# Layer 0 of a modulated convolution in five matmuls instead of six, with the next block's first half copied into a stacked buffer

## The chip, the cores and the metric

The kernel runs on one core of one Trainium2 chip. The metric is the device time of one launch in microseconds (us). The engines are TensorE (PE; its weight loads are shown apart as PEld), VectorE (DVE), ScalarE (ACT), GpSimd (POOL) and SyncE (SP, which here only issues transfers).

## What is computed

The input `x` is (128 samples, 32 channels, 512 positions). It goes through four modulated 1-D convolutions (3 taps, 32 to 32 channels), then through a mixture of experts with a shared expert, and is added to the result. Cut to what matters here:

```python
TYPES = ('same', 'upsample', 'same', 'downsample')
def _conv_same(x, w):
    p = (K - 1) // 2
    return lax.conv_general_dilated(x[None], w, (1,), [(p, p)], ...)[0]
def _layer(x, style, w, b, mw, mb, typ):
    s = style @ mw.T + mb
    weight = SCALE * w * s[:, None, :, None]
    demod = lax.rsqrt(jnp.sum(weight * weight, axis=(2, 3)) + EPS)
    weight = weight * demod[:, :, None, None]
    if typ == 'same':
        out = jax.vmap(_conv_same)(x, weight) + b[None, :, None]
...
x = x + _L0_ffn_ref(_L0_cond_ref(x, cond_512, ...), ...)   # 16 experts, top 4 of each row, and a shared expert
```

The layer of the change is the first one, of type "same": each output position takes the three input positions around it.

## The kernel before

**Tiling.** The 4096 rows (sample, channel) are cut into G = 32 blocks of 128 rows, which are four samples of 32 channels. For the convolutions the 512 positions of a row are split by their remainder modulo Q = 4. The 128 partitions then hold four groups of 32 channels, one for each remainder, and the free dimension holds 4 samples of V = 128 positions each. In this layout a convolution is a matmul with a 128x128 matrix of placed taps: in layer 0 the matrix `FIRST` takes the inputs of the same group of four positions, and `FIRST + 1` takes those of the following group (the data shifted by one column). Of this second matrix only the rows of the first two remainders, partitions 0 to 63, hold taps.

**Two parts.** All operands of TensorE are split into a high and a low part (`x0[0]`, `x0[1]` for the data, `cwt[0]`, `cwt[1]` for the taps), and a product is three matmuls: high by high, high data by low taps, low data by high taps. Layer 0 therefore takes six matmuls of 128x512 for each block (`hi_passes` issues four, `lo_passes` two). The data's high part is made by ACT (`first_in`, L586, out of `xraw`), its low part by DVE (`first_in`, L840).

**Order.** Each engine runs its own program, `body(g)` for g = 0 to 33, and semaphores tie them together. In body g of PE stand, in this order: layer 0 of block g+1, the transposes of block g-2's rows, layer 1 of block g, layer 3 of block g-1, the shared expert's first product, layer 2 of block g, then the router's logits and the shared expert's second product. For the last six blocks the shared expert is put off until the convolutions are through. ACT takes each layer out of its bank (L592) and makes the high part of block g+2's input; DVE makes the low parts. Layer 0 of block 0 and layer 0 of block 1 have nothing of a block before them; block 1's stands in body 0. In body 0 DVE also mixes the taps of the last layer (`mixture`, L865 and L867), which ACT copies (L572) ahead of its evacuation of layer 2.

**SP's queue.** SP issues nearly all transfers, in one order. In body g: an output block (L377) and a load of `xbase` (L379), four copies that stack layer 0's result for layer 1 (L362), four writes of the finished rows `h_rows` (L385), and the load of `xraw` for block g+3 (L390). An instruction that waits on SP holds up all that stand behind it. Ahead of the bodies SP waits until layer 1's input of block 0 is stacked, and then loads `xraw` of block 2 (L370). In body 1 it also loads the first expert's weights, 1.5 MB (L396, L397).

After the convolutions the experts' jobs run, with TensorE at work nearly all the time to the end.

The functions that the diff touches, and what calls them:

Of the kernel before, what the change touches and what calls it, by code (L numbers as in the profile page):

```python
# [5 lines left out]
P = 128  # L6
F32 = mybir.dt.float32
# [10 lines left out]
def mk_adaln_ffn(nc, x, xq, styleT, taps, placed_taps, small, modT, gateT, Wup, Wdn, Sup, Sdn, out):  # L18
# [46 lines left out]
    with ExitStack() as ctx:  # L65

        def sb(name, shape, dt=F32):
            buffer = ctx.enter_context(nc.sbuf_tensor(name, shape, dt))
            size = 2 if dt == BF16 else 4
            for n in shape[1:]:  # L70
                size *= n
            if 0 < size % 64 <= 32:
                ctx.enter_context(nc.sbuf_tensor(f"{name}_gap", [P, 8], F32))
            return buffer

        def sem(name):
# [56 lines left out]

        x0 = [sb("x0_hi", [P, NB, VP], F32R), sb("x0_lo", [P, NB, VP], F32R)]

        x1p = sb("x1p", [P, 2, NB, V], F32R)


# [62 lines left out]
        names = ("style_loaded taps_loaded placed_loaded0 placed_loaded1 placed_loaded2 bias_loaded gate_loaded iota_done consts_done dve_step mixed_ready pos_ready "  # L201
                 "s_psum wts_hi wts_lo dem_psum sqrt_done eps_ready s_ready s2_ready scales_ready "
                 "raw_loaded w_hi w_lo fill_written "
                 "x_loaded0 x_loaded1  base_loaded0 base_loaded1 x0_hi x0_lo "
                 "l0_done l1_done l2_done l3_done t1_ready t2_ready t3_ready h_ready "
                 "x1_ready x1_stacked x2_ready x3_ready xt_t xt_hi xt_lo up_done sg_ready z_ready "
                 "logits_done sig_ready mask_ready prefix_done place_ready zt_t zt_hi zt_lo down_done "
# [65 lines left out]
        def within(g, least, most):  # L273
            return not isinstance(g, int) or least <= g < most
# [59 lines left out]
        def _(sp):  # L334
# [17 lines left out]
            def stack(g, plane_=None):  # L352
# [4 lines left out]
                for plane, to, part, rows, back in PLACES:  # L357
                    if plane_ is not None and plane != plane_:
# [3 lines left out]
                    sp.dma_start(x1[C * to:C * (to + rows), :, :, plane, dst].rearrange("p a b u -> p (a b) u").bitcast(F32),  # L362
                                 x1p[C * part:C * (part + rows), :, :, src].rearrange("p a b u -> p (a b) u").bitcast(F32)).then_inc(S["x1_stacked"], 16)

            stack(0, 0)
            sp.wait_ge(S["x0_hi"], 1)
            sp.wait_ge(S["x0_lo"], 1)

            sp.wait_ge(S["x1_stacked"], 16 * STACKS)
            sp.dma_start(xraw[:, 0], xq[2]).then_inc(S["x_loaded0"], 16)  # L370

            def body(g, it, u):

                odd = g % 2 if u is None else (R + 1 + u) % 2
                if within(g, 3, G - LATE + 3):
                    sp.wait_ge(S["o_ready"], g - 2)
                    sp.dma_start(out[bass.ds(P * (g - 3), P), :], orow[:, 1 - odd, :]).then_inc(S[f"o_written{1 - odd}"], 16)  # L377
                    if within(g, 3, G + 1):
                        sp.dma_start(xbase[:, 1 - odd, :], x_rows[bass.ds(P * (g - 1), P), :]).then_inc(S[f"base_loaded{1 - odd}"], 16)  # L379
                if within(g, 0, G - 1):  # L380
                    stack(g + 1)
                if within(g, 1, G + 1):
                    sp.wait_ge(S["h_ready"], g)
                    for q in range(Q):
                        sp.dma_start(h_rows[bass.ds(P * (g - 1), P), q * (L // Q):(q + 1) * (L // Q)].rearrange("(b c) w -> c b w", b=NB),  # L385
                                     hrow[C * q:C * q + C, 1 - odd]).then_inc(S[f"h_written{1 - odd}"], 16)
                if within(g, 0, G - 3):
                    sp.wait_ge(S["x0_hi"], g + 2)
                    sp.wait_ge(S["x0_lo"], g + 2)
                    sp.dma_start(xraw[:, 1 - odd], xq[bass.ds(g + 3, 1)].rearrange("a p b v -> p (a b) v")).then_inc(S[f"x_loaded{1 - odd}"], 16)  # L390
                if isinstance(g, int) and g == 1:
                    sp.wait_ge(S["w_lo"], HC + IC)
                    load_expert(0)
# [363 lines left out]
        def _(dve):  # L757
# [71 lines left out]
            def matrix_lo(n):  # L829
                src, at, to, m = MATRICES[n]  # L830
                dve.wait_ge(S["wts_hi"], n + 1 + n // 3)
                minus(cwt[1][:, to:to + m], src[:, at:at + m], cwt[0][:, to:to + m]).then_inc(S["wts_lo"], 1)

            def minus(lo, src, hi):
                return dve.tensor_tensor(lo, src, hi.bitcast(F32), ALU.subtract)  # L835
# [129 lines left out]
            def body(g, it, u):  # L965
# [49 lines left out]
                    dve.tensor_tensor(z[:, 0, :], z[:, 0, :], bank[6][:, I:2 * I], ALU.mult).then_inc(S["z_ready"], 1)  # L1015
                if many:
                    settle(number, many)
                if early and g == G + 1:
                    late_z(G - LATE)
                if is_late(g):  # L1020
# [2 lines left out]
                    routing()  # L1023
                if early and g == 0:
                    mixture(1, 3, PLACED_DOWN, BK, "placed_loaded2", step)
                if within(g, 0, G - 2):
                    first_in(g + 2, odd)
                for ph in range(2):
                    if ph == 1 and shared:
                        dve.wait_ge(S["zt_hi"], g - 1)  # L1030
# [185 lines left out]
        def _(pe):  # L1216
# [29 lines left out]
            def layer0(g):  # L1246
                if isinstance(g, int) and g == 0:
                    pe.wait_ge(S["wts_lo"], 1)
                else:
                    pe.wait_ge(S["t1_ready"], g)  # L1250
                dst = bank[0][:].rearrange("p (b v) -> p b v", b=NB)
                same = [columns(FIRST + m, P, lambda a: x0[a][:, :, m:m + V]) for m in range(2)]
                pe.wait_ge(S["x0_hi"], g + 1)
                hi_passes(pe, dst, same)
                pe.wait_ge(S["x0_lo"], g + 1)
                lo_passes(pe, dst, same).then_inc(S["l0_done"], 1)

            def prefix(number, many):

# [240 lines left out]
def _laid_out(inputs):  # L1500
# [24 lines left out]
        return a.reshape(P, P)  # L1525

    turned = cw.transpose(0, 2, 1, 3)
    placed = [place(turned[0], lambda q, j: j + Q * m - q) for m in range(2)]
    placed += [place(turned[2], lambda q, j: j + Q * m - q - 1) for m in range(2)]
    placed += [place(cw[1], lambda q, j: 1 - 2 * j + q + n) for n in range(4)]  # L1530
    placed += [place(turned[3], lambda q, j: j + Q * m - 2 * q - n) for n in range(4) for m in range(3)]
# [36 lines left out]
```

## Time and profile before

| | |
|---|---|
| median of 3 runs | 1179.65 us (1178.35 to 1181.12) |
| the profiled execution | 1181.02 us, of which the profile's span is 1179.3 us |
| TensorE busy with matmuls | 1122.3 us, 95% |
| VectorE / ScalarE / GpSimd busy | 798.0 / 515.3 / 538.0 us |
| convolution stage | from the start to about 470 us |

The profiled execution is 1.37 us above the median. Its time outside the span is 1.7 us. Busy shares are averages over two stages that differ, so the rows below are read by stretch.

### The profile page before, as it was taken

The page shows a single profiled execution, that of the slowest core. Times are in us where ns is not written, and L with a number is a line of the kernel's source. Part 1 is how long each engine was busy: PE and PEld are TensorE (multiplying, and loading weights), DVE is VectorE, ACT ScalarE, POOL GpSimd, SP SyncE. Part 2 cuts the span into 40 slices and gives each one's busy share as a digit, 9 for nine tenths or more (in the row PEclk, how much of TensorE's full clock was granted, in tenths as well). Part 3 has the DMA queues.
Part 4 walks back from the last instruction along what each step waited for, and adds up shares of the span by engine and source line. Part 5 has one row for each costly group of instructions (what it writes and reads, how often), then busy time and mean ns, then how long its engine had stood idle before and what let it go on. Part 6 is the DMA issues. An engine that isn't in the chain of part 4 may idle for free. (4 is left out here: it accounts for less than half of the span.)

```text
span 1179.3 us, 24615 instructions
## 1 busy us (share of the span) xinstructions
PE 1122.3 (95%) x7157; PEld 1006.7 (85%) x7158; DVE 798.0 (68%) x2057; ACT 515.3 (44%) x1246; POOL 538.0 (46%) x639
## 2 busy tenths in 40 slices
PE   5899999999999978889999999999999999999995
PEld 4788888888888866679999999999997999999995
DVE  7988887888888875745655656556567565555653
ACT  5776666666666653132323333223234232232321
POOL 1000131322222364545566566665655556566663
PEclk8999999999999998979999999999999999999998
DMA  7655555555555541367766776767667776666664
GB/s 253 179 158 157 148 157 158 156 154 143 143 153 152 152 111 44 106 163 147 153 129 114 156 121 125 152 115 154 119 154 160 153 161 122 111 112 109 115 114 71
DMA packets 140255, 163.66 MB, mean 139 GB/s; under 512 B 31456, under 2 KB 97088, under 8 KB 138688
## 3 DMA queue, kind: packets, MB, share of 16 engines
q0 software_dynamic: 36000, 75.39, 35.3%
q1 hardware_dynamic: 102832, 87.06, 25.2%
q10 hardware_dynamic: 1392, 0.85, 0.3%
q8 instruction: 13, 0.21, 0.1%
q14 instruction: 18, 0.15, 0.0%
HBM read 74.58 MB, written 55.18 MB: 110 GB/s over the span
## 5 line engine op out<-in xcount | busy, mean ns | idle before, releaser
L1468 PE MATMUL bank<-xt_hi,wup_hi 128*128 128x256 f32 x1104 | 278.4, 284 | 1.9 <-ACT xt_hi L716 1.5
L1468 PE MATMUL bank<-xt_hi,wup_lo 128*128 128x256 f32 x1104 | 278.1, 284 | 0.0
L445 POOL DMA_INDIRECT lists<-entry,place x128 | 126.0, 984 | 326.8 <-DVE x_lo L835 266.4
L501 POOL DMA_INDIRECT out_rows<-placed,sid x140 | 226.6, 1619 | 90.9 <-DVE placed L1188 66.8
L592 ACT ACTIVATE t<-bank,cB,cA 128x256 f32<-128x256 f32 (+1 forms) x384 | 175.9, 535 | 96.7 <-PE bank L231 89.7
L1468 PEld LDWEIGHTS bank<-xt_hi,wup_hi 128*128 128x128 f32 x1104 | 212.6, 193 | 6.4 <-issue 2.0
L1468 PEld LDWEIGHTS bank<-xt_hi,wup_lo 128*128 128x128 f32 x1104 | 212.9, 193 | 2.5
L486 POOL DMA_INDIRECT placed<-h_rows,gid x140 | 141.5, 1011 | 120.7 <-PE bank L1446 78.2
L1472 PE MATMUL bank<-xt_lo,wup_hi 128*128 128x256 f32 x1104 | 178.3, 284 | 0.0
L1188 DVE TENSOR_SCALAR placed<-bank,all_lists 128x512 f32<-128x512 f32 x138 | 99.8, 748 | 87.0 <-DMA out_rows<-placed,sid 55.2
L733 ACT ACTIVATE zt_hi<-z 128x256 fp32r<-128x256 f32 x138 | 57.6, 418 | 231.0 <-DVE z L1178 231.0
L1472 PEld LDWEIGHTS bank<-xt_lo,wup_hi 128*128 128x128 f32 x1104 | 153.2, 193 | 0.0
L729 ACT ACTIVATE sg<-bank 128x256 f32<-128x256 f32 x138 | 52.4, 380 | 211.6 <-PE bank L1472 211.4
L1484 PE MATMUL bank<-wdn_hi,zt_hi 128*128 128x512 f32 x276 | 114.6, 415 | 2.3 <-ACT zt_hi L733 2.3
L1486 PE MATMUL bank<-wdn_hi,zt_lo 128*128 128x512 f32 x276 | 108.4, 393 | 0.0
L224 PE MATMUL bank<-x_hi,cwt_hi 128*128 128x512 f32 (+1 forms) x256 | 100.3, 395 | 8.3 <-DVE x_hi L1008 3.1
L1484 PE MATMUL bank<-wdn_lo,zt_hi 128*128 128x512 f32 x276 | 107.3, 389 | 0.0
L835 DVE TENSOR_TENSOR zt_lo<-z,zt_hi 128x256 fp32r<-128x256 f32 x138 | 58.8, 426 | 61.9 <-ACT zt_hi L733 61.9
L1178 DVE TENSOR_TENSOR z<-z,bank 128x256 f32<-128x256 f32 x138 | 58.2, 422 | 62.4 <-PE bank L1472 60.9
L224 PE MATMUL bank<-x_hi,cwt_lo 128*128 128x512 f32 (+1 forms) x256 | 99.6, 389 | 0.0
L1160 DVE TENSOR_TENSOR xt_lo<-bank,xt_hi 128x512 fp32r<-128x512 f32 x140 | 90.3, 686 | 11.1 <-ACT xt_hi L716 7.0
L231 PE MATMUL bank<-x_lo,cwt_hi 128*128 128x512 f32 (+2 forms) x384 | 95.2, 355 | 0.0
(258 smaller groups left out, 2088.8 us busy)
## 6 DMA issues: line engine op xcount, KB each, us to landing
x<-x1p SPq DMA_DIRECT2D x63, 384.0 KB
wraw<-in_Wup SPq DMA_DIRECT2D x11, 1024.0 KB, 7.8
xraw<-in_xq SPq DMA_DIRECT2D x32, 260.0 KB, 2.7
xbase<-in_x SPq DMA_DIRECT2D x32, 256.0 KB, 2.8
h_rows<-hrow SPq DMA_DIRECT2D x128, 64.0 KB
x<-x1p SPq DMA_DIRECT2D x63, 127.0 KB
out_rows<-orow SPq DMA_DIRECT2D x30, 256.0 KB, 2.1
wdraw<-in_Wdn SPq DMA_DIRECT2D x11, 512.0 KB, 9.9
```

Source lines behind the costliest of these rows:

```text
L224: r = pe.matmul(dst, lhs[a if data_moves else 0], rhs[0 if data_moves else a], start=n == 0 and a == 0, stop=False)
L231: r = pe.matmul(dst, lhs[0 if data_moves else 1], rhs[1 if data_moves else 0], start=False, stop=last and n == len(terms) - 1)
L445: pool.indirect_dma_start(out=lists, out_offset=bass.IndirectOffsetOnAxis(ap=place[:, home, r, k:k + 1], axis=0), in_=entry[:, home, r, k, ...
L486: pool.indirect_dma_start(out=xg[:, u, :], out_offset=None, in_=h_rows, in_offset=bass.IndirectOffsetOnAxis(ap=gid[:, u:u + 1], axis=0)).t ...
L501: pool.indirect_dma_start(out=out, out_offset=bass.IndirectOffsetOnAxis(ap=sid[:, u:u + 1], axis=0), in_=yb[:, u, :], in_offset=None, comp ...
L592: r = act.activation(dst[:, n], src[:, n], ACT.Identity, scale=cA[:, l, bass.ds(g * NB + b, 1)], bias=cB[:, l, bass.ds(g * NB + b, 1)])
L1160: dve.tensor_tensor(xt[1][:, u].rearrange("p c t -> p (c t)"), bank[4 + u][:], xt[0][:, u].rearrange("p c t -> p (c t)").bitcast(F32), ALU ...
L1188: dve.tensor_scalar(yb[:, u, :], bank[6 + u][:], all_lists[:, bass.ds(at + u, 1), 1], None, ALU.mult).then_inc(S["b_y"], 1)
L1468: pe.matmul(dst, lhs[a], rhs[0], start=k == 0 and a == 0, stop=False)
L1472: r = pe.matmul(dst, lhs[0], rhs[1], start=False, stop=k == HC - 1)
L1484: pe.matmul(bank[6 + u][:], zt[0][:, u, c, :], wdn[b][a][:, c, :], start=c == 0 and a == 0, stop=False)
L1486: r = pe.matmul(bank[6 + u][:], zt[1][:, u, c, :], wdn[b][0][:, c, :], start=False, stop=c == IC - 1)
```

## The change

Layer 0 of blocks 1 to 31 takes five matmuls instead of six; block 0 keeps six.

- The taps of the following group, which lay in rows 0 to 63 of `cwt[..][:, FIRST + 1]`, are now placed in rows 64 to 127 too, for the high part. In the low part rows 64 to 127 are set to zero by a memset on DVE.
- A new buffer `x0n` holds partitions 0 to 63 of the data's high part in its lower half, and partitions 0 to 63 of its low part in its upper half. One matmul of it with the high taps then does what two did: high by high and low by high of the following group.
- `x0n` is filled by SP with two copies from SBUF to SBUF for each block, of 64 partitions by 520 elements (2080 bytes) each, 130 KB. The first waits for the high part, the second for the low part (`stack_next`). For block 1 they stand behind the load of `xraw` at L370, for block g+2 behind the load of `xraw` in body g. The last matmul of layer 0 waits for them.
- DVE's `first_in(g + 2)` is issued earlier in its body: ahead of `mixture` in body 0, and ahead of `gathered` in bodies 28 and 29. In other bodies nothing that DVE issues stands between the old place and the new.

```diff
@@ SP @@
+            def stack_next(g):
+                for a, part in enumerate(("x0_hi", "x0_lo")):
+                    sp.wait_ge(S[part], g + 1)
+                    sp.dma_start(x0n[a * (P // 2):(a + 1) * (P // 2)].rearrange("p b v -> p (b v)").bitcast(F32),
+                                 x0[a][0:P // 2].rearrange("p b v -> p (b v)").bitcast(F32)).then_inc(S["x0_stacked"], 16)
...
             sp.wait_ge(S["x1_stacked"], 16 * STACKS)
             sp.dma_start(xraw[:, 0], xq[2]).then_inc(S["x_loaded0"], 16)
+            stack_next(1)
...
                     sp.dma_start(xraw[:, 1 - odd], xq[bass.ds(g + 3, 1)].rearrange("a p b v -> p (a b) v")).then_inc(S[f"x_loaded{1 - odd}"], 16)
+                if within(g, 0, G - 2):
+                    stack_next(g + 2)
@@ DVE @@
-                minus(cwt[1][:, to:to + m], src[:, at:at + m], cwt[0][:, to:to + m]).then_inc(S["wts_lo"], 1)
+                r = minus(cwt[1][:, to:to + m], src[:, at:at + m], cwt[0][:, to:to + m])
+                if n == 0:
+                    link(r)
+                    r = dve.memset(cwt[1][P // 2:P, FIRST + 1, :].bitcast(F32), 0.0)
+                r.then_inc(S["wts_lo"], 1)
...
+                if within(g, 0, G - 2):
+                    first_in(g + 2, odd)
                 if early and g == G + 1:
                     late_z(G - LATE)
                 if is_late(g):
...
                 if early and g == 0:
                     mixture(1, 3, PLACED_DOWN, BK, "placed_loaded2", step)
-                if within(g, 0, G - 2):
-                    first_in(g + 2, odd)
@@ PE, layer0 @@
-                same = [columns(FIRST + m, P, lambda a: x0[a][:, :, m:m + V]) for m in range(2)]
+                here = columns(FIRST, P, lambda a: x0[a][:, :, 0:V])
+                following = columns(FIRST + 1, P // 2, lambda a: x0[a][0:P // 2, :, 1:V + 1])
                 pe.wait_ge(S["x0_hi"], g + 1)
-                hi_passes(pe, dst, same)
-                pe.wait_ge(S["x0_lo"], g + 1)
-                lo_passes(pe, dst, same).then_inc(S["l0_done"], 1)
+                if isinstance(g, int) and g == 0:
+                    hi_passes(pe, dst, [here, following])
+                    pe.wait_ge(S["x0_lo"], g + 1)
+                    lo_passes(pe, dst, [here, following]).then_inc(S["l0_done"], 1)
+                else:
+                    hi_passes(pe, dst, [here])
+                    pe.matmul(dst, cwt[1][:, FIRST + 1, :], x0[0][:, :, 1:V + 1], start=False, stop=False)
+                    pe.wait_ge(S["x0_lo"], g + 1)
+                    lo_passes(pe, dst, [here], last=False)
+                    pe.wait_ge(S["x0_stacked"], g * 32)
+                    pe.matmul(dst, cwt[0][:, FIRST + 1, :], x0n[:, :, 1:V + 1], start=False, stop=True).then_inc(S["l0_done"], 1)
```

How it stands on the engines at three places. First PE, layer 0 of block 1 and the first matmul of layer 1 of block 0 behind it (`x_hi`, `x_lo` are the two parts of block 1's data, `x` is the stacked input of layer 1), before:

```order
L224 MATMUL bank<-x_hi,cwt_hi 128x512 [waits x0_hi,t1_ready]
L224 MATMUL bank<-x_hi,cwt_lo 128x512
L224 MATMUL bank<-x_hi,cwt_hi 128x512
L224 MATMUL bank<-x_hi,cwt_lo 128x512
L231 MATMUL bank<-x_lo,cwt_hi 128x512 [waits x0_lo]
L231 MATMUL bank<-x_lo,cwt_hi 128x512
L224 MATMUL bank<-x,cwt_hi 128x512 [waits iota_done,x1_stacked,sqrt_done,wts_lo]
```

And the same place in the changed program:

```order
L227 MATMUL bank<-x_hi,cwt_hi 128x512 [waits x0_hi,t1_ready]
L227 MATMUL bank<-x_hi,cwt_lo 128x512
L1281 MATMUL bank<-x_hi,cwt_lo 128x512
L234 MATMUL bank<-x_lo,cwt_hi 128x512 [waits x0_lo]
L1285 MATMUL bank<-x0n,cwt_hi 128x512 [waits x0_stacked]
L227 MATMUL bank<-x,cwt_hi 128x512 [waits iota_done,x1_stacked,sqrt_done,wts_lo]
```

Six matmuls have become five, and the fifth waits for the copies; layer 1 stands behind it.

Second SP, from the load of `xraw` ahead of the bodies (the first row) through body 0, before:

```order
L370 DMA xraw<-in_xq 128x520 [waits x1_stacked,x0_lo,x0_hi]
L362 DMA x<-x1p 96x8x128 [waits l1_done,x1_ready]
L362 DMA x<-x1p 32x8x127
L362 DMA x<-x1p 96x8x128
L362 DMA x<-x1p 32x8x127
L390 DMA xraw<-in_xq 128x520 [waits x0_lo,x0_hi]
```

In the changed program:

```order
L381 DMA xraw<-in_xq 128x520 [waits x1_stacked,x0_lo,x0_hi]
L373 DMA x0n<-x_hi 64x520 [waits x0_hi]
L373 DMA x0n<-x_lo 64x520 [waits x0_lo]
L365 DMA x<-x1p 96x8x128 [waits l1_done,x1_ready]
L365 DMA x<-x1p 32x8x127
L365 DMA x<-x1p 96x8x128
L365 DMA x<-x1p 32x8x127
L402 DMA xraw<-in_xq 128x520 [waits x0_lo,x0_hi]
L373 DMA x0n<-x_hi 64x520 [waits x0_hi]
L373 DMA x0n<-x_lo 64x520 [waits x0_lo]
```

Each load of `xraw` now has the two copies right behind it, and the later bodies repeat this.

Third DVE in body 0, the end of layer 1's evacuation, the mixture, and the low part of block 2's input (`x_lo<-xraw`), before:

```order
L835 TENSOR_TENSOR x_lo<-t,x_hi 128x4x128 [waits x2_ready]
L865 TENSOR_SCALAR mixed<-placed 128x384 [waits placed_loaded2]
L867 SCALAR_TENSOR_TENSOR mixed<-placed,mixed 128x384 [waits dve_step] x3
L840 SCALAR_TENSOR_TENSOR x_lo<-xraw,s,x_hi 128x130 [waits x0_hi]
L840 SCALAR_TENSOR_TENSOR x_lo<-xraw,s,x_hi 128x130 x3
L1046 MEMSET t 64x2 [waits t3_ready]
```

In the changed program:

```order
L853 TENSOR_TENSOR x_lo<-t,x_hi 128x4x128 [waits x2_ready]
L858 SCALAR_TENSOR_TENSOR x_lo<-xraw,s,x_hi 128x130 [waits x0_hi]
L858 SCALAR_TENSOR_TENSOR x_lo<-xraw,s,x_hi 128x130 x3
L883 TENSOR_SCALAR mixed<-placed 128x384 [waits placed_loaded2]
L885 SCALAR_TENSOR_TENSOR mixed<-placed,mixed 128x384 [waits dve_step] x3
L1064 MEMSET t 64x2 [waits t3_ready]
```

The four instructions on block 2's input have moved ahead of the four that mix the taps.

## Rows read from the trace of the kernel before

**Rows 1.** Busy time by stretch: PE, PEld, DVE, ACT, POOL, PEclk, DMA, GB/s

```profile
20.00:40.00 20.00, 12.68 (x49) 9.20 (x48) 17.09 (x47) 12.25 (x31) 2.86 (x4) 0.83 0.45 133
60.00:80.00 20.00, 20.00 (x103) 16.79 (x102) 15.90 (x40) 15.92 (x39) 0.00 (x0) 1.00 0.56 156
...
420.00:440.00 20.00, 13.68 (x71) 11.09 (x69) 15.88 (x67) 12.21 (x31) 11.38 (x13) 0.91 0.29 73
```

**Rows 2.** Timeline of PE, one block's layer 0: start, us, line, tiles

```profile
210.89 0.40 PE L224 MATMUL bank<-x_hi,cwt_hi 128*128 128x512 f32 x1
...
211.83 0.63 PE L231 MATMUL bank<-x_lo,cwt_hi 128*128 128x512 f32 x2
...
224.70 0.40 PE L224 MATMUL bank<-x_hi,cwt_hi 128*128 128x512 f32 x1
```

**Rows 3.** Timeline of SP, the same block

```profile
207.53 0.37 SPq L390 DMA_DIRECT2D xraw<-in_xq  x1
213.02 0.36 SPq L377 DMA_DIRECT2D out_rows<-orow  x1
213.56 0.35 SPq L379 DMA_DIRECT2D xbase<-in_x  x1
```

**Rows 4.** Transfers by line: issues, KB each, median us from issue to landing

```profile
xraw<-in_xq SPq DMA_DIRECT2D x32, 260.0 KB, 2.7
xbase<-in_x SPq DMA_DIRECT2D x32, 256.0 KB, 2.8
...
out_rows<-orow SPq DMA_DIRECT2D x30, 256.0 KB, 2.1
...
out_rows<-zrow POOLq DMA_DIRECT2D x2, 256.0 KB, 3.0
```

**Rows 5.** Timeline of SP and PE, the block with the shortest such distance

```profile
291.40 0.37 SPq L390 DMA_DIRECT2D xraw<-in_xq  x1
...
295.35 0.63 PE L231 MATMUL bank<-x_lo,cwt_hi 128*128 128x512 f32 x2
```

**Rows 6.** Timelines of SP, PE, ACT and DVE, body 0

```profile
22.70 0.35 SPq L370 DMA_DIRECT2D xraw<-in_xq  x1
...
22.73 0.47 PE L224 MATMUL bank<-x,cwt_hi 128*128 128x512 f32 x1 [2.70 <-DMA x<-x1p]
...
23.93 3.33 ACT L592 ACTIVATE t<-bank,cB,cA 128x128 f32<-128x128 f32 x8 [2.64 <-DVE tsum L821]
...
25.47 0.43 DVE L852 CAST x1p<-t 128x512 fp32r<-128x512 f32 x1 [1.69 <-ACT t L592]
...
31.23 0.52 ACT L572 ACTIVATE cwt_hi<-mixed 128x384 fp32r<-128x384 f32 x1 [2.81 <-DVE mixed L867]
```

**Rows 7.** Timeline of DVE and PE from body 0's end into body 1

```profile
31.12 1.14 DVE L840 SCALAR_TENSOR_TENSOR x_lo<-xraw,s,x_hi 128x130 fp32r<-128x130 f32 x4
32.73 0.06 DVE L1046 MEMSET t<- 64x2 f32 x1 [0.47 <-ACT t L592]
...
40.10 0.50 PE L224 MATMUL bank<-x_hi,cwt_hi 128*128 128x512 f32 x1 [1.01 <-DVE x_hi L1008]
```

**Rows 8.** Timeline of SP and PE, body 1's end and body 2's start

```profile
44.37 0.64 PE L231 MATMUL bank<-x_lo,cwt_hi 128*128 128x512 f32 x2
...
44.87 0.40 SPq L390 DMA_DIRECT2D xraw<-in_xq  x1
...
45.71 0.47 PE L224 MATMUL bank<-x,cwt_hi 128*128 128x512 f32 x1 [0.27 <-DMA x<-x1p]
```

**Rows 9.** Timeline of SP, PE, ACT and DVE, body 29, layer 0 of block 30

```profile
416.39 0.38 SPq L390 DMA_DIRECT2D xraw<-in_xq  x1
...
417.47 0.64 PE L231 MATMUL bank<-x_lo,cwt_hi 128*128 128x512 f32 x2
...
418.25 2.42 ACT L592 ACTIVATE t<-bank,cB,cA 128x128 f32<-128x128 f32 x6 [0.29 <-PE bank L231]
...
421.59 0.42 DVE L852 CAST x1p<-t 128x512 fp32r<-128x512 f32 x1
```

More of the change, by code:

```diff
@@ L134, in mk_adaln_ffn @@
         x0 = [sb("x0_hi", [P, NB, VP], F32R), sb("x0_lo", [P, NB, VP], F32R)]
+        x0n = sb("x0n", [P, NB, VP], F32R)
         x1p = sb("x1p", [P, 2, NB, V], F32R)
@@ L203, in mk_adaln_ffn @@
                  "raw_loaded w_hi w_lo fill_written "
-                 "x_loaded0 x_loaded1  base_loaded0 base_loaded1 x0_hi x0_lo "
+                 "x_loaded0 x_loaded1  base_loaded0 base_loaded1 x0_hi x0_lo x0_stacked taps_cut "
                  "l0_done l1_done l2_done l3_done t1_ready t2_ready t3_ready h_ready "
@@ L1527, in _laid_out @@
     turned = cw.transpose(0, 2, 1, 3)
-    placed = [place(turned[0], lambda q, j: j + Q * m - q) for m in range(2)]
+    placed = [place(turned[0], lambda q, j: j - q), place(turned[0], lambda q, j: j % (Q // 2) + Q - q)]
     placed += [place(turned[2], lambda q, j: j + Q * m - q - 1) for m in range(2)]
```

## The prediction, made before the changed kernel ran

> **What bounds the kernel now.** I read the busy time by stretch first. In the convolution stage from 60 us on TensorE is busy for the whole of each stretch at full clock, 20.00 of 20.00 us, with VectorE at 15.90 [rows 1]. The timeline of TensorE shows the same from near: one block's layer 0 starts at 210.89, the next block's at 224.70, a period of 13.81 us with no idle time noted in it [rows 2]. There a matmul less is time less. Not so at both ends of the stage: from 20 to 40 us TensorE is busy for 12.68 us of 20 and VectorE for 17.09, and from 420 to 440 us it is 13.68 against 15.88 [rows 1]. In those stretches a chain through ScalarE and VectorE sets the time. TensorE is the bound again in the experts' stage, which the change doesn't touch, so that what the convolutions gain or lose is passed on whole.
>
> **What is removed.** Four matmuls of 128x512 go from 210.89 to 211.83, 0.235 us from start to start [rows 2]. (The 0.40 us in the row is one matmul's own duration, and they overlap.) The matmul is removed 31 times. It counts where TensorE is saturated: from body 2 (layer 0 of block 3), since the last waits of TensorE that VectorE sets end at 40.10 us [rows 7], to body 28 (block 29). These are 27 blocks, -6.3 us. The first two and last two lie where other engines are waited for, and count nothing.
>
> **What is added on SP, and when it lands.** Two issues of some 0.36 us stand behind each load of `xraw` [rows 3]. They delay nothing on SP in a block's middle: the next instruction there, at 213.02, waits for its output block 5 us after the load at 207.53 [rows 3]. What matters is when the data is there. The trace has no such copy of 64 partitions, so I bound it by neighbours of the same size. A load of `xraw` lands 2.7 us after its issue [rows 4]. The pair of copies, 260 KB, is issued within the next 1.1 us, and follows it in one queue. How long 260 KB take behind another transfer is seen at the output and `xbase`: issued at 213.02 and 213.56 [rows 3], they land 2.1 and 2.8 us later [rows 4], at 215.12 and 216.36, which is 1.24 us for 256 KB. So the pair lands 2.7 + 1.26 = 3.96 us after the issue of `xraw`. Bounds: no time at all behind the load (2.7), and each half as dear as a whole one (5.2). I take 3.96, as the bytes are the same.
>
> The Trainium skill (DMA: Bandwidth & Descriptors, section on the anatomy of one DMA) gives about 2.0 us fixed for a transfer and one microsecond for each 436 KB beyond it. By that the pair would follow the load after some 0.6 us instead of 1.26, and each of the three waits that I price below would be that much shorter, some 1.8 us off my sum. The trace's neighbours are slower than that, and I go by them.
>
> **The middle blocks.** The fifth matmul starts where the fifth did before, four matmuls after layer 0's start: at 211.83, 4.30 us after the load at 207.53 [rows 2, 3]. Against 3.96 that leaves 0.3 us. In the block with the least room it is 291.40 to 295.35, 3.95 us [rows 5]: nothing left. It is the shortest of 24 blocks in which I read this distance. I take 0.4 us in all for the tight ones. With bounds of 2.7 and 5.2 us it would be none, or 0.9 us in each.
>
> **The start, block 1.** Before, layer 0 of block 1 was done long before it was wanted: ScalarE took it at 23.93, and what it had waited for was a scale of VectorE's [rows 6]. Now its last matmul waits for the pair behind the load at 22.70: 26.7 us. GpSimd's fills start at that time as well and need 3.0 us each [rows 4]; sharing the engines could cost up to 1.3 us. I take 27.1. ScalarE starts 0.54 us after the last of two matmuls (417.47 + 0.24, then 418.25) [rows 9], so at 27.6 instead of 23.93: +3.7 us (3.3 to 4.5). Layer 1 of block 0, which ran from 22.73 [rows 6], stands behind it on TensorE. VectorE waits for that evacuation already, 1.69 us at 25.47 [rows 6], and from there on is busy almost without a gap until TensorE waits for it at 40.10 [rows 7]. So this reaches the saturated part.
>
> **The start, VectorE's order.** Block 2's low part takes 1.14 us at 31.12, right behind the mixture [rows 7]. It lay in the shade of ScalarE's copy of the mixed taps, which had waited 2.81 us for the mixture, from 31.23 [rows 6], and of the evacuation behind it, for which VectorE still waits 0.47 us at 32.73 [rows 7]. Put ahead of the mixture, it delays the mixture, the copy, the evacuation and VectorE's next work: +1.1 us, on the same chain. The memset (one of 64x128 elements) comes ahead of a matmul that waits for data anyway: nothing, and at most its 0.1 us.
>
> **Body 2, block 3.** Here the room is negative. The load of `xraw` in body 1 is issued at 44.87, when layer 0 of block 3 has already reached its fifth matmul (44.37) [rows 8]. The pair lands at 44.87 + 3.96 = 48.83: 4.46 us of TensorE waiting, of which 0.27 us were waited behind it before, at 45.71 [rows 8]. +4.2 us. Both sides shift alike with the start, so this adds up. In body 3 the delay itself gives SP time to catch up.
>
> **Body 29, block 30.** The late blocks are short on TensorE, without the shared expert: the load at 416.39, the fifth matmul at 417.47 [rows 9]. The pair lands at 420.35, 2.9 us late. But VectorE takes the result only at 421.59, and ScalarE has the first four of its six pieces done by about 419.85 [rows 9]: 1.7 us of room. +1.1 us. Block 31's copies are late too, by less than that room.
>
> **The clock.** TensorE runs at 2.4 GHz where the row shows 1.00. In 20 to 40 us, with over 7 us idle, the mean granted clock is 0.83, and in 420 to 440 it is 0.91 [rows 1]: time at the lower level, 1.2 GHz, that costs (1 - 0.91) x 20 = 1.8 us there. A wait of over 4 us in body 2, with a saturated stretch behind it, should bring one such fall where each matmul counts: +1.8 us, nothing to 3.4 us (the loss of the first stretch).
>
> **The sum.** 3.7 + 1.1 + 4.2 + 1.1 + 0.4 + 1.8 - 6.3 = +6.0 us. On the profiled execution's own 1181.02 us that is 1187.0; it stood 1.4 us above the median of the runs, so against 1179.65 I forecast **1185.6 us**, slower by 0.5%.
>
> **Rivals.**
> - *The clock holds and the copies are quick.* Without the fall, with 3.3 us at the start and a pair that follows the load after half of the 1.26 us, within its bounds, so 0.6 us less in body 2 and at the end: 3.3 + 1.1 + 3.6 + 0.5 - 6.3 = +2.2, 1181.9 us, on the edge of no change. For it: from 60 us on the clock is full in all that I read of the middle, so it takes some idle time to bring it down. Against it: over 4 us of it in one piece.
> - *The delays outside the saturated stretch are absorbed* (the other side). TensorE waits for others from 20 to 40 and from 420 on [rows 1]; if there is slack in the chain that I haven't seen, block 1's wait, VectorE's order and block 30's wait cost nothing, and the clock falls no further than it did. Left are 4.2 - 6.3 = -2.1, 1177.5 us; it ends faster once the pair in body 2 lands 0.3 us sooner. Against it: VectorE's 17.09 of 20 us [rows 1], and its wait at 25.47 that grows with ScalarE's [rows 6].
> - *Every block stalls.* If a half-width copy is as dear as a whole one, the pair lands 5.2 us after the load, 0.9 us late in each of 25 blocks: +22 us. Already 4.7 us would cost 0.4 each, +10: some 1196 us. For it: the thin room of 0 to 0.3 us. Against it: same bytes, same number of engines by the neighbours.
> - *The change doesn't do what it says*: it does, five matmuls stand in each block's row of the order.
>
> **Chances.** Forecast 0.60 (1183 to 1190), the clock holding 0.20, absorbed 0.08, every block stalling 0.12. About 0.2% (2.4 us) is what a measurement of this kernel can tell from none. Faster by more than that, under 1177.3: 0.07, most of the absorbed case. Within it: 0.21, most of the clock holding and the rest of the absorbed. Slower: 0.72. The range from 1178.5 to 1193 leaves out the better part of the absorbed case and of the stalling one.
>
> **What would show it.** TensorE's last layer-0 matmul, the one that reads `x0n`, should have idle time ahead of it put down to a transfer: some 7 us in body 0, over 4 us in body 2, near 3 us in body 29, and tenths at most between. The first matmul of layer 2 in body 1, before at 40.10, should start near 45, and the period of a middle block should be 13.57 instead of 13.81. Between 45 and 60 us the granted clock should be under 1.00 in some stretch. A period at or above 13.81 would prove the stalling rival; a first matmul at 40 to 41 us the absorbed one.

## The result, and the profile after

The changed kernel takes 1204.23 us (median of 4 runs, 1201.26 to 1207.1). Beside it, on the same chip, the kernel before took 1180.38 us (median of 4, the fastest 1178.35; one of its four runs, at 1572.04, was disturbed and is left out of the ratio, and the other three have the median 1179.65). The ratio is 1.0192, with a 95% interval of 1.0171 to 1.0212: **slower by 1.9%**, where 0.5% was forecast. The time lies outside the predicted range. The profiled execution took 1202.69 us, span 1200.8.

TensorE's waits in the whole convolution stage (0 to 470 us) of the changed kernel. A row gives the engine and line, what was waited for, the us in total, how many times, and the longest:

```profile
PE bank L1285 <- DMA x0n<-x_lo: 35.3, 25, 9.1
PE bank L1238 <- DMA styt<-in_styleT: 4.9, 1, 4.9
```

L1285 is the new last matmul of layer 0, the one that reads `x0n`. It waits 25 times, 35.3 us in all. Its five large waits, in the timeline of TensorE (blocks 1, 2, 3, 30 and 31):

```profile
28.31 0.80 PE L1285 MATMUL bank<-x0n,cwt_hi 128*128 128x512 f32 x1 [9.14 <-DMA x0n<-x_lo]
...
40.85 0.50 PE L1285 MATMUL bank<-x0n,cwt_hi 128*128 128x512 f32 x1 [3.92 <-DMA x0n<-x_lo]
...
56.87 0.80 PE L1285 MATMUL bank<-x0n,cwt_hi 128*128 128x512 f32 x1 [5.78 <-DMA x0n<-x_lo]
...
446.36 0.50 PE L1285 MATMUL bank<-x0n,cwt_hi 128*128 128x512 f32 x1 [3.35 <-DMA x0n<-x_lo]
...
460.71 0.50 PE L1285 MATMUL bank<-x0n,cwt_hi 128*128 128x512 f32 x1 [3.02 <-DMA x0n<-x_lo]
```

They make 25.2 us; the other 20 waits share 10.1. Those 20 are the surprise. Here is one of them: SP and TensorE around layer 0 of block 15, which answers to [rows 2, 3]:

```profile
220.03 3.33 SPq L365 DMA_DIRECT2D x<-x1p  x4
223.54 2.71 SPq L397 DMA_DIRECT2D h_rows<-hrow  x4
226.59 0.37 SPq L402 DMA_DIRECT2D xraw<-in_xq  x1
227.02 0.51 SPq L373 DMA_DIRECT2D x0n<-x_hi  x1
227.58 0.59 SPq L373 DMA_DIRECT2D x0n<-x_lo  x1
...
229.23 0.40 PE L227 MATMUL bank<-x_hi,cwt_hi 128*128 128x512 f32 x1
...
229.94 0.40 PE L234 MATMUL bank<-x_lo,cwt_hi 128*128 128x512 f32 x1
230.63 0.50 PE L1285 MATMUL bank<-x0n,cwt_hi 128*128 128x512 f32 x1 [0.29 <-DMA x0n<-x_lo]
230.96 0.27 PE L1337 MATMUL bank<-ident,hrow 128*128 128x128 f32 x1
```

From the load's issue to the start that the fifth matmul would have had (229.94 + 0.235 = 230.17) there are 3.58 us; the prediction had 4.30. The matmul started 4.04 us after the issue. The block loses more than the 0.29 us that the row notes. The note counts from the end of the matmul before (229.94 + 0.40), not from the start that the next would have had, and the matmul behind the stacked one starts late as well: 229.94 to 230.96 is 1.02 us where two starts take 0.47, a loss of 0.55.

What came closer is the load itself, since the run of issues ahead of it on SP became longer. Such a run in the kernel before, of the block after that of [rows 3]:

```profile
215.64 2.78 SPq L362 DMA_DIRECT2D x<-x1p  x4
218.52 2.56 SPq L385 DMA_DIRECT2D h_rows<-hrow  x4
221.33 0.37 SPq L390 DMA_DIRECT2D xraw<-in_xq  x1
```

From the first stacked copy to the load it takes 5.69 us in the kernel before and 6.56 in the changed one (medians over the stage: 5.7 and 6.5).

To see which part of the stage lost what, I took the first matmul of layer 0 of blocks 4 and 29. Before:

```profile
58.14 0.40 PE L224 MATMUL bank<-x_hi,cwt_hi 128*128 128x512 f32 x1
...
405.56 0.40 PE L224 MATMUL bank<-x_hi,cwt_hi 128*128 128x512 f32 x1
```

After:

```profile
72.09 0.40 PE L227 MATMUL bank<-x_hi,cwt_hi 128*128 128x512 f32 x1
...
430.93 0.40 PE L227 MATMUL bank<-x_hi,cwt_hi 128*128 128x512 f32 x1
```

| | forecast | measured |
|---|---|---|
| up to block 4 | +10.6 us | +14.0 (72.09 - 58.14) |
| block 4 to block 29, 25 periods | -5.5 us | +11.4 (358.84 - 347.42) |
| from there to the end of the span | +0.9 us | -3.9 (what is left of 1200.8 - 1179.3 = 21.5) |

The forecast column adds the terms of the prediction: 3.7 + 1.1 + 4.2 + 1.8 less one matmul; 25 matmuls less and 0.4 for the tight blocks; 1.1 less one matmul. The span is 21.5 us longer where +6.0 were forecast. The middle row is 16.9 us over its forecast, more than this whole error of 15.5; the first row adds 3.4, and the last is 4.8 under its forecast, which lies within what the stage behind it varies by, as the part on what is left open says.

### The profile page after: what moved, and what is told of

It is laid out like the page before. It is cut to its first block and busy times, and to the rows that moved or that the text cites. A ratio compares the mean times of both kernels' runs of the same rounds, so it can differ in the third digit from the quotient of the medians.

```text
span 1200.8 us, 24636 instructions
## 1 busy us (share of the span) xinstructions
PE 1123.5 (94%) x7126; PEld 993.9 (83%) x7127; DVE 799.3 (67%) x2058; ACT 515.2 (43%) x1246; POOL 538.3 (45%) x639
## 5 line engine op out<-in xcount | busy, mean ns | idle before, releaser
L1497 PE MATMUL bank<-xt_hi,wup_hi 128*128 128x256 f32 x1104 | 274.3, 281 | 1.8 <-ACT xt_hi L730 1.5
L1497 PE MATMUL bank<-xt_hi,wup_lo 128*128 128x256 f32 x1104 | 273.4, 280 | 0.0
L1497 PEld LDWEIGHTS bank<-xt_hi,wup_hi 128*128 128x128 f32 x1104 | 208.3, 189 | 6.6 <-ACT xt_hi L730 1.9
L1497 PEld LDWEIGHTS bank<-xt_hi,wup_lo 128*128 128x128 f32 x1104 | 208.2, 189 | 3.0
L1501 PE MATMUL bank<-xt_lo,wup_hi 128*128 128x256 f32 x1104 | 175.2, 280 | 0.0
L1501 PEld LDWEIGHTS bank<-xt_lo,wup_hi 128*128 128x128 f32 x1104 | 149.9, 188 | 0.0
L227 PE MATMUL bank<-x_hi,cwt_hi 128*128 128x512 f32 (+1 forms) x225 | 89.1, 400 | 4.7 <-ACT x_hi L600 2.0
L853 DVE TENSOR_TENSOR x_lo<-t,x_hi 128x512 fp32r<-128x512 f32 x128 | 88.9, 695 | 3.7
L1193 DVE TENSOR_TENSOR z<-sg,bank 128x256 f32<-128x256 f32 x138 | 57.7, 418 | 47.4 <-ACT sg L743 43.8
```

The source lines that it names most:

```text
L227: r = pe.matmul(dst, lhs[a if data_moves else 0], rhs[0 if data_moves else a], start=n == 0 and a == 0, stop=False)
L1497: pe.matmul(dst, lhs[a], rhs[0], start=k == 0 and a == 0, stop=False)
L1501: r = pe.matmul(dst, lhs[0], rhs[1], start=False, stop=k == HC - 1)
```

## The experiments

Each ratio is to runs of the kernel before on the same chip, with its 95% interval. "4 to 29" is the stretch between the two matmuls above, in each kernel's own trace.

**1. Only the buffer.** The kernel before, with `x0n` declared where the change has it, and never used.

```diff
+        x0n = sb("x0n", [P, NB, VP], F32R)
         x1p = sb("x1p", [P, 2, NB, V], F32R)
```

> The kernel before with nothing but an unused buffer of x0n's size allocated at x0n's place. It moves x1p, x1 and hrow up by 2112 bytes, so that x1p goes from a multiple of 256 bytes to one plus 64. Theory A (address): the 512-byte pieces of the stacking copies and of the row writes get dearer by this alone, and SP's run from the first stacking copy to the load of xraw in a middle block grows from 5.7 us towards the changed kernel's 6.6 us; TensorE doesn't wait for them here, so the time stays within 0.3% of before (1178 to 1184 us). Theory B (traffic): only the two copies themselves slow the queue, so here that run stays at 5.7 us and the time at 1180 us.

1182.72 us (10 runs), ratio 1.0005 [0.9992, 1.0018]. But its transfers did change. The hardware queue between 100 and 400 us, as packets, MB and share of the 16 engines' time, in the kernel before:

```profile
q1 hardware_dynamic: 66959, 45.20, 53.6%
```

with the unused buffer:

```profile
q1 hardware_dynamic: 66050, 44.75, 58.9%
```

and its SP:

```profile
216.78 3.28 SPq L364 DMA_DIRECT2D x<-x1p  x4
220.17 2.79 SPq L387 DMA_DIRECT2D h_rows<-hrow  x4
223.21 0.37 SPq L392 DMA_DIRECT2D xraw<-in_xq  x1
```

Fewer bytes in more time, and a run of 6.43 us instead of 5.69. `x0n` takes 2080 bytes of each partition and a gap of 32 that the helper `sb` adds, together 2112, which is 8 x 256 + 64. So `x1p`, `x1`, the rows' buffers and all others behind it are shifted by 64 bytes against the multiples of 256, and `x1p`, which the stacked copies read, goes from a multiple of 256 to 64 past one. A packet of 512 bytes takes 35.1 ns in this trace and 29.9 before, one of 508 bytes 34.5 and 28.8 (means of some 43,000 and 11,000 packets between 100 and 400 us). Nothing in this kernel waits on that run, and the time of the whole shows nothing of it. The stretch from block 4 to block 29 does show something:

```profile
58.43 0.40 PE L226 MATMUL bank<-x_hi,cwt_hi 128*128 128x512 f32 x1
...
407.73 0.40 PE L226 MATMUL bank<-x_hi,cwt_hi 128*128 128x512 f32 x1
```

4 to 29 takes 349.30 us instead of 347.42, and the period of a middle block is 13.90 us instead of 13.81, with no wait noted. Nearly all of that lies in the shared expert's first product (2.80 us instead of 2.73 in block 15). These 1.9 us are below what the ratio of the whole can tell, and what slows TensorE there was not looked into.

The dearer packets fit the Trainium skill (DMA: Bandwidth & Descriptors, section on how a descriptor splits into AXI transactions): a piece that doesn't start at a multiple of 256 bytes has its first transaction started at the boundary below, and the bytes fetched in vain still cost time. By that, 512 bytes from 64 to 576 cost 18 beats (steps of 32 bytes) instead of 16, an estimate of 1.13 times; the trace has 1.17.

**2. The buffer elsewhere.** The changed kernel, `x0n` declared behind all other buffers. It is called kernel 2 below.

```diff
-        x0n = sb("x0n", [P, NB, VP], F32R)
         x1p = sb("x1p", [P, 2, NB, V], F32R)
...
+        x0n = sb("x0n", [P, NB, VP], F32R)
```

> The changed kernel with x0n allocated behind all other buffers, so that these stand where they stood before. Theory A (address): SP's run is back at 5.7 us, the wait for x0n in a middle block goes from 0.4-0.5 us to under 0.1, the period of a block from 14.2 to about 13.7 us; 25 blocks by 0.45 us give 11 us, so some 1192 us. Theory B (traffic): nothing changes, 1204 us.

1190.94 us, 1.0071 [1.0046, 1.0097]: more than half of the loss is gone with one line moved. SP's run is 5.8 us, packets of 512 bytes 29.9 ns. 4 to 29: 346.9 us, read in the slowest of its five runs (1197.02 us).

**3. The buffer padded.** The changed kernel with `x0n` in its place, and 192 bytes behind it, so that the others start at a multiple of 256 again.

```diff
         x0n = sb("x0n", [P, NB, VP], F32R)
+        fill = sb("fill", [P, 48])
```

> The changed kernel, x0n where the change puts it, with 192 unused bytes in each partition behind it, so that x1p and all buffers behind it start again at a multiple of 256 bytes. Theory A, that the buffers' addresses being 64 bytes off a multiple of 256 makes the transfers of 508 and 512 bytes slow: as the kernel with x0n at the end, ratio 1.005 to 1.010, 512-byte packets at some 30 ns and SP's stretch from the first stacked copy to the load of xraw at 5.8 us. Rival, that another thing of the place counts: ratio 1.019, 35 ns and 6.5 us.

1193.52 us, 1.0095 [1.0063, 1.0126]; run 5.7 us, 29.9 ns; 4 to 29: 347.7 us. So it is the 64 bytes, not the place. A middle block of it:

```profile
220.22 0.37 SPq L403 DMA_DIRECT2D xraw<-in_xq  x1
...
224.38 0.40 PE L235 MATMUL bank<-x_lo,cwt_hi 128*128 128x512 f32 x1
224.62 0.40 PE L1286 MATMUL bank<-x0n,cwt_hi 128*128 128x512 f32 x1
```

The room from the load's issue to the fifth matmul is back at 4.40 us, and this block doesn't wait. Others still do: in runs 2 and 3 the stacked matmul of tight blocks starts 0.1 to 1.5 us late, and both kernels still take 347 us or more for the stretch, where 25 matmuls less should leave 341.5.

**4. The copies ahead of the load.** Kernel 2, with each body's copies issued before the load of `xraw`.

```diff
+                if within(g, 0, G - 2):
+                    stack_next(g + 2)
                 ...load of xraw for block g + 3...
-                if within(g, 0, G - 2):
-                    stack_next(g + 2)
```

> The changed kernel with x0n placed behind all other buffers and, in each body, SP's two copies ahead of the load of xraw instead of behind it. Theory A, that what is left of the loss is waiting for copies that queue behind a load: the waits of the middle blocks, 0.1 to 1.5 us, go, the pair lands a microsecond sooner in body 2 and the late ones too, together 4 to 6 us less than the kernel with the buffer alone moved (ratio 1.0071): 1184 to 1187 us beside a before of 1180. Rival, that the load of xraw, now later, makes ScalarE's and VectorE's first halves late: 1190 us or more.

1187.7 us, 1.0049 [1.0033, 1.0065]. No middle block waits any more. TensorE's waits for `x0n` in the stage:

```profile
PE bank L1285 <- DMA x0n<-x_lo: 14.2, 4, 8.8
```

and the ends of its stretch:

```profile
69.30 0.40 PE L227 MATMUL bank<-x_hi,cwt_hi 128*128 128x512 f32 x1
...
411.06 0.40 PE L227 MATMUL bank<-x_hi,cwt_hi 128*128 128x512 f32 x1
```

341.76 us, 5.66 less than before: 0.226 us for each of the 25 matmuls. The load, now later, costs nothing.

**5. Copies that nobody reads.** Two kernels. The first keeps six matmuls, with the copies of blocks 1 to 30 issued and `x0n` in the change's place, the following group on 64 rows (its matrix has taps in the other 64 that must not count twice):

```diff
...the two branches of layer 0, five matmuls and six, become one...
+                hi_passes(pe, dst, [here, following])
+                pe.wait_ge(S["x0_lo"], g + 1)
+                lo_passes(pe, dst, [here, following]).then_inc(S["l0_done"], 1)
```

> The changed kernel, x0n in its place, with six matmuls in layer 0 of all blocks as before; the copies of blocks 1 to 30 are still issued, but no matmul reads them (ScalarE waits for the copies of the block before ahead of overwriting x0, which have landed by then except for block 2's). Both theories: SP's run stays long, but TensorE waits for no copy. If it is the wait for the copies that costs (my account), the time is 1181 to 1184 us. If the transfers themselves take something from the other engines, it stays above 1190 us.

1197.74 us, 1.0124 [1.009, 1.0158]. That looked as if the copies cost 15 us by themselves. But layer 0 itself had become longer, so this kernel changes two things at once, and I separated them. The second keeps the six matmuls of 128 rows, `x0n` behind all others, the copies issued for blocks 1 to 30:

> The kernel before, six matmuls of 128 rows, with x0n placed behind all other buffers and both copies of each of blocks 1 to 30 issued as in the changed kernel; nothing reads x0n. Theory A, that what the change costs is the waiting for the copies and not their traffic: 1180 to 1184 us. Rival, that the copies' issues and bytes on SP's queue slow the other transfers and the blocks with them: SP's stretch from the first stacked copy to the load of xraw longer than 5.8 us, and 1186 us or more.

1180.33 us (10 runs), 0.9991 [0.9974, 1.0008], and SP's run stays at 5.7 us. In this kernel the copies' traffic and issues are free; waiting for them is not.

**6. 64 rows, and nothing else.** The kernel before, one line changed. The rows it leaves out hold no taps in this matrix, so nothing of the computation is missing (the expectation has this wrong).

```diff
-                same = [columns(FIRST + m, P, lambda a: x0[a][:, :, m:m + V]) for m in range(2)]
+                same = [columns(FIRST, P, lambda a: x0[a][:, :, 0:V]), columns(FIRST + 1, P // 2, lambda a: x0[a][0:P // 2, :, 1:V + 1])]
```

> The kernel before with one line changed: the second tap of layer 0 takes only the first 64 rows of its matrix and of its data (the upper taps' share of the second tap is left out). No copies, no new buffer. Theory A, that a matmul of 64 rows beside matmuls of 128 rows costs 0.4 to 0.5 us more per block (layer 0 from 1.4 to some 2.1 us in the copies-unused kernel): 32 x 0.5 = +16 us, some 1196 us, and all of the loss of the copies-unused kernel. Theory B, that this loss came from the copies and the new buffer: within 1179 to 1183 us.

1198.94 us, 1.0142 [1.0121, 1.0163]: all of the first kernel of run 5. Its layer 0 on TensorE, and the weight loads:

```profile
219.04 0.40 PE L224 MATMUL bank<-x_hi,cwt_lo 128*128 128x512 f32 x1
219.38 0.50 PE L224 MATMUL bank<-x_hi,cwt_hi 64*128 64x512 f32 x1
219.72 0.40 PE L224 MATMUL bank<-x_hi,cwt_lo 64*128 64x512 f32 x1
```

```profile
219.38 0.18 PEld L224 LDWEIGHTS bank<-x_hi,cwt_hi 64*128 64x128 f32 x1 [0.38 <-issue]
219.49 0.19 PEld L224 LDWEIGHTS bank<-x_hi,cwt_lo 64*128 64x128 f32 x1
220.05 0.19 PEld L231 LDWEIGHTS bank<-x_lo,cwt_hi 128*128 128x128 f32 x1 [0.38 <-issue]
```

A matmul of 64 rows starts 0.34 us after its neighbour instead of 0.235 [rows 2]. The first weight load of 64 rows comes no earlier than its own matmul, at 219.38, instead of under the one before; the load after the change back to 128 rows, at 220.05, is as late. The second load of 64 rows, at 219.49, does lie under the matmul before it. In these rows the overlap is lost where the row count changes. The changed kernel is spared this, because its stacked matmul has 128 rows; only its block 0 has it.

**7. VectorE's order undone.** Kernel 2, `first_in(2)` in body 0 behind the mixture again.

```diff
-                if within(g, 0, G - 2):
+                if within(g, 1, G - 2):
                     first_in(g + 2, odd)
...mixture...
+                    first_in(2, 0)
```

> The changed kernel with x0n placed behind all other buffers, and in body 0 VectorE's work for block 2's first half again behind the mixture of the taps, as in the kernel before. Theory A, that the order costs what the prediction took, 1.1 us on the chain to layer 2 of block 1: 1189.8 us against 1190.9 of the kernel with the buffer alone moved, and the first matmul of layer 2 in body 1 some 1.1 us sooner. Rival, that block 2's wait for its copies hides it or grows with it: no difference, or slower, since block 2's own halves come later.

1191.31 us, 1.0083 [1.0063, 1.0103], which the interval doesn't tell from kernel 2. The traces do: the first matmul of layer 2 in body 1, in kernel 2

```profile
45.67 0.50 PE L227 MATMUL bank<-x_hi,cwt_hi 128*128 128x512 f32 x1 [1.02 <-DVE x_hi L1026]
```

and with the order undone

```profile
44.63 0.50 PE L227 MATMUL bank<-x_hi,cwt_hi 128*128 128x512 f32 x1 [1.02 <-DVE x_hi L1026]
```

1.04 us sooner, as the term of 1.1 said, and block 4's layer 0 starts 1.0 us sooner too. For the whole time this stays below what the runs tell.

**8. Six matmuls at both ends.** Kernel 2, with the six (on 64 rows) in blocks 1 to 3, 30 and 31, made before run 6 had shown what these cost.

```diff
-                if isinstance(g, int) and g == 0:
+                if isinstance(g, int) and not 4 <= g <= 29:
```

> As e2 (x0n behind all buffers), and blocks 1, 2, 3, 30 and 31 take six matmuls and no copies; 4 to 29 take five. The three long waits of the start and the two of the end go. If these are what is left of the loss, the result is 26 blocks by -0.235 us, +1.1 us for VectorE's order in body 0, and under 1 us of waits in the middle: 1175 to 1177 us. If the middle blocks still wait 0.4 us each it is 1185 us.

1187.36 us (10 runs), 1.0044 [1.0023, 1.0065]. Inconclusive as a price of the ends, for the 64 rows are in it; and block 4 waits 4.04 us, its copies standing behind the first expert's weights on SP.

**9. Five matmuls only where TensorE is saturated.** The copies ahead of the load, `x0n` behind the others, VectorE's order as before, and a matrix of stacked taps of its own, so that the other blocks keep six matmuls of 128 rows. Blocks 6 to 29:

```diff
-                if isinstance(g, int) and g == 0:
+                if isinstance(g, int) and not 6 <= g <= 29:
...
-                    pe.matmul(dst, cwt[0][:, FIRST + 1, :], x0n[:, :, 1:V + 1], ...)
+                    pe.matmul(dst, cwt[0][:, NM, :], x0n[:, :, 1:V + 1], ...)
```

> Five matmuls in blocks 6 to 29 alone, by a matrix of stacked taps of their own; the others have the six matmuls of 128 rows of the kernel before. x0n is placed behind all other buffers, the copies are issued ahead of the load of xraw, and VectorE's order in body 0 is that of before. Theory A, that a matmul less is 0.235 us where TensorE is saturated and that the rest of the loss is waiting for copies and the buffer's place: 24 x 0.235 = 5.6 us less, 1174.5 to 1177 us. Rival, that removing a matmul from a middle block gives nothing back: 1180 us or more.

1176.5 us, 0.9956 [0.9937, 0.9976]: faster than both kernels, and 5.2 us less than before where 24 x 0.235 = 5.6 were expected. The same with blocks 30 and 31 as well:

> As the kernel with five matmuls in blocks 6 to 29 (1176.5 us), but blocks 30 and 31 take five too. Theory A, that the end of the stage waits for the copies of these two, 3.35 and 3.02 us in the changed kernel, somewhat less with the copies ahead of the load: +1 to +3 us, 1178 to 1179.5 us. Rival, that ScalarE and VectorE are behind there anyway and nothing of it counts: 1176 to 1177 us.

1176.54 us, 0.9958 [0.9939, 0.9978], the same. Blocks 30 and 31 do wait for their copies:

```profile
415.19 0.51 PE L1285 MATMUL bank<-x0n,cwt_hi 128*128 128x512 f32 x1 [1.58 <-DMA x0n<-x_lo]
...
428.50 0.50 PE L1285 MATMUL bank<-x0n,cwt_hi 128*128 128x512 f32 x1 [2.42 <-DMA x0n<-x_lo]
```

but nothing of it reaches the end, so the rival won. Against this kernel, the one of run 4 differs by five matmuls in blocks 1 to 5, VectorE's order, the 64 rows in block 0 and the stacked taps' own matrix, all of them at the start: 1.0049 against 0.9958 is 10.7 us. The traces put it there too: block 4's layer 0 starts at 69.30 in run 4's kernel and at 58.46 in this one.

## Why the prediction was wrong, point by point

**The middle blocks: the step that failed.** "The fifth matmul starts where the fifth did before, 4.30 us after the load" took SP's timetable from the trace of before, and "0.4 us in all for the tight ones" followed. Measured, 25 periods lost 358.84 - (347.42 - 5.9) = 17.3 us. Of these, 15.5 are lost at the stacked matmul, counted in each block as in block 15 above; the rows note only 9.7 of them as waits, in 19 of the 25 blocks. The 1.8 that are left match TensorE's slower pace in run 1 (1.9 there). By cause there are two parts, shown apart:

- *The buffer's size, 11 to 12 us of the stretch* (358.8 against 346.9 and 347.7), 0.97 to 1.21% in the ratios. The prediction costed the copies and the matmul but not the declaration. It moved every later buffer by 64 bytes past a multiple of 256, the pieces of the stacked copies and the rows' writes took 17% longer, SP came to the load 0.8 us later, and of 4.30 us of room some 3.7 were left (median of the 25 blocks). Some 1.9 us of this part cost no wait at all, by run 1.
- *The queue behind the load, 5 to 6 us* (346.9 and 347.7 against 341.8). The estimate of the landing was good: in kernel 2 the second copy lands 3.1 us after its issue (median), which is 1.0 us behind the load's, so 4.1 where I had 3.96. Its spread was left out. With the old addresses, in the blocks of kernel 2 that wait, the matmul starts 3.8 to 4.5 us after the load's issue, where I had 3.96 for all; and the room, 3.95 to 4.30, is spread over the same values. I had treated nought to 0.3 us as a margin; some ten of the 25 blocks came late.

"Every block stalls" came nearest in time, at 1196 us, and still too low: it had 0.4 us for each block where 0.69 were lost (17.3 / 25). Its sign came true as well, since the mean period is 14.35 us (358.84 / 25), above the 13.81 that the prediction named as its proof. But that sign tells only that the middle blocks lose time, not why. The rival's mechanism, a half copy as dear as a whole one (5.2 us), is not what the traces show: the pair landed where I had it, but the load ahead of it was issued late.

The figures that the prediction cites from the Trainium skill (DMA: Bandwidth & Descriptors, section on the anatomy of one DMA) are given there for transfers that GpSimd issues. By them 130 KB would take 2.3 us, an estimate; the copies here, issued by SP behind a load, took 3.1 (run 2, median).

**What is removed: right.** 0.226 us for each matmul in run 4, 5.2 us for 24 in run 9, against 0.235 each.

**The start, block 1: too small.** I took 27.1 us for the last matmul and +3.7 us for ScalarE; it was 28.31, and ScalarE began at 29.23 instead of 23.93 [rows 6], +5.3:

```profile
23.17 0.35 SPq L381 DMA_DIRECT2D xraw<-in_xq  x1
...
29.23 3.52 ACT L606 ACTIVATE t<-bank,cB,cA 128x128 f32<-128x128 f32 x8 [8.19 <-PE bank L1285]
...
30.77 0.43 DVE L870 CAST x1p<-t 128x512 fp32r<-128x512 f32 x1 [7.01 <-ACT t L606]
```

The load was issued 0.47 us later than before, the pair landed 5 us after it, which is my upper bound (5.2) and not the 3.96, and ScalarE followed 0.92 us after the start of that matmul where I had 0.54. With VectorE's order (1.1, shown as 1.04) that makes 6.4, and the trace has just that: layer 2 of body 1 starts at 46.47 instead of 40.10 [rows 7]. The chain was read rightly.

**Body 2, block 3: right in kind, +5.5 instead of +4.2.** The wait is 5.78 us, 0.27 of which replace the wait of [rows 8]. The issue of the load took 1.41 us there instead of 0.40 [rows 8], and the copies' issues stood behind it:

```profile
51.98 1.41 SPq L402 DMA_DIRECT2D xraw<-in_xq  x1
53.44 0.50 SPq L373 DMA_DIRECT2D x0n<-x_hi  x1
```

**The clock: right.** One fall where matmuls count. It begins inside the wait of 5.78 us (51.1 to 56.9 us), between 55.0 and 55.5, and ends between 62.0 and 62.3. Busy time by stretch, as in [rows 1]; the eighth number from the left, after the five engines, is the granted clock:

```profile
46.00:55.00 9.00, 5.02 (x27) 3.65 (x25) 7.73 (x22) 4.60 (x12) 0.00 (x0) 1.00 0.74 176
55.50:62.00 6.50, 5.13 (x14) 4.17 (x15) 2.10 (x6) 3.56 (x9) 0.00 (x0) 0.50 0.76 260
62.30:70.00 7.70, 7.70 (x45) 6.57 (x43) 4.42 (x13) 5.32 (x13) 0.00 (x0) 1.00 0.92 218
```

0.50 is the level of 1.2 GHz. (Another fall, from 41.8 to 45.1 us with a granted clock of 0.51, behind the wait of 3.92, lies in the start, as the one between 20 and 40 us did before; in that stretch the granted clock now stays at 1.00, on which the last section has a word.) Block 3's last matmul stands 12.3 us later than before (6.4 + 5.5 and the wait's own restart), block 4's first 14.0: some 1.7 us for the fall, 1.8 forecast.

**Body 29, block 30: of no account.** The waits came, 3.35 and 3.02 us. That they cost 1.1 us is not seen; run 9 shows that for the better kernel they cost nothing.

**The absorbed rival** has nothing for it: its sign was a first matmul of layer 2 at 40 to 41 us, which started at 46.47, and the 10.7 us of the start are in the medians of run 4 against run 9.

Left open: how the span gives back 3.9 us behind block 29. From there to the end, seven traces (the changed kernel, and runs 2, 3, 4, 7 and 9) vary between 4.9 us less than before and 3.7 more, and repeated runs of the kernel before spread over 6 to 8 us on one chip (1178.72 to 1184.35, 1178.18 to 1186.47), so a single profile doesn't decide it. I didn't follow it. Nor is it known why TensorE's pace in the shared expert's product changes with the buffer.

## What to carry to other kernels

A new buffer has an address, and so have all that are declared behind it: before adding one, see whether its size keeps the others on the multiple of 256 bytes on which their 512-byte transfers start, or put it last. A distance read from the trace of before is only as firm as every issue ahead of it on the same queue; where the margin is smaller than its scatter from block to block, price a wait in a good part of the blocks, by starts and not by the noted idle time, and issue the urgent copy ahead of the load that nobody waits for. Saving a matmul by a transfer pays only where the engine is saturated and the data is early: 24 of 31 blocks gave all of the gain, and the first five, with what else changed at the start, cost twice that.

## What the runs showed of the hardware that I had not expected

- 64 bytes of address: packets of 512 bytes 29.9 to 34.9 ns, of 508 bytes 28.8 to 34.3, in the changed kernel; 29.9 and 28.7 again with 192 bytes of padding.
- A matmul with 64 rows of weights among ones of 128 rows costs more than one of 128: 0.34 us from start to start instead of 0.235, and 0.43 for the last two of layer 0. Layer 0 takes 2.10 us (218.81 to 220.91) instead of 1.41, and the kernel 17 us more over 32 blocks.
- With the unused buffer of run 1, which shifts the others by 64 bytes, TensorE's middle blocks take 13.90 us instead of 13.81, with no wait noted. The cause is open.
- 130 KB copied from SBUF to SBUF over 64 partitions, behind a load of 260 KB, land 2.8 to 2.9 us after their issue, as the load itself does (2.9), in the kernel that issues copies beside six matmuls.
- A granted clock of 1.00 in the record doesn't say that matmuls start 0.235 us apart right after idle time: from 28.90 to 31.03, behind 9.14 us of waiting, they start 0.43 us apart, where the stretch from 28 to 31 us has

```profile
28.00:31.00 3.00, 2.69 (x6) 2.17 (x7) 0.23 (x1) 1.77 (x5) 0.00 (x0) 1.00 0.18 74
```
